# Key rows of a routed attention: one-hot products on TensorE replaced by indirect DMAs driven by token lists

## What is computed

```
s = xn + sum over 8 heads of relu(causal scores)/512 @ V      (stage A)
local = windowed attention, 16 heads of 64, windows of 64      (stage B)
per window w = 1..7, per group g = 0, 1:                       (stage C)
    score the 64*w earlier tokens, keep the 128 best (router: 20 descent steps, then top_k)
    score the window's own 64 tokens, keep the 32 best as queries
    routed = x[b, sel_idx]                   # the selected rows
    out = attention(queries, [null key] + routed rows), 16 heads
    scatter-add out to the queries' tokens
y = (local + scattered) / counts
out = x + s * silu(y)
```

## Time and profile before

| | |
|---|---|
| median of 3 runs | 795.33 us (795.16 to 795.91) |
| profiled execution | 795.43 us, of which the traced span is 793.6 us |
| PE busy | 751.6 us, 95% of the span |
| DVE / ACT / POOL busy | 458.8 / 431.0 / 233.0 us |
| chain that ended last | PE 86%, ACT 5%, DVE 4% |
| granted TensorE clock, mean | 0.991 |
| `a_diag`, `a_v` on DVE (L1512, L1507), mean of 32 each | 692 ns, 692 ns |
| a unit of stage A in head 6, from PE's first scores to the next (174.97 to 181.11) | 6.14 us |
| the query round's two operations (56x64), mean | 224 and 208 ns |

### The profile page before, as it was taken

One profiled execution on the slowest core, in us unless ns is written; L12 is line 12 of the kernel. 1 busy time (PEld: TensorE's weight loads), 2 busy tenths in 40 slices (PEclk: granted clock), 3 DMA queues, 4 the chain that ended last, 5 costly groups with the idle time before them and its releaser, 6 DMA issues.

```text
span 793.6 us, 18031 instructions
## 1 busy us (share of the span) xinstructions
PE 751.6 (95%) x6307; PEld 589.4 (74%) x6311; DVE 458.8 (58%) x1028; ACT 431.0 (54%) x1575; POOL 233.0 (29%) x373
## 2 busy tenths in 40 slices
PE   3799999999999899999999999799999999999996
PEld 3587888878877566666666678687878788787875
DVE  6422333356645788777777752756564555656454
ACT  2254444432223567777766773666474656647562
POOL 1320000000003797554554421422223222212301
PEclk9999999999999999999999998999999999999999
DMA  8600000000001323333333310000000000000001
GB/s 242 273 1 2 0 0 0 0 0 0 0 1 44 92 58 85 91 76 77 76 81 80 76 37 1 1 1 1 0 0 0 1 1 2 1 0 0 0 1 54
DMA packets 22543, 28.87 MB, mean 36 GB/s; under 512 B 6224, under 2 KB 12880, under 8 KB 21840
## 3 DMA queue, kind: packets, MB, share of 16 engines
q1 hardware_dynamic: 22480, 28.04, 12.9%
HBM read 10.19 MB, written 1.05 MB: 14 GB/s over the span
## 4 chain that ended last, share of the span: by engine, by line
PE 86%; ACT 5%; DVE 4%; SPq 2%; issue 2%; POOL 1%; DVEq 0%; DMA 0%; POOLq 0%; ACTq 0%
PE ps L710 9%; PE ps L698 8%; PE ps L759 7%; PE ps L973 6%; PE ps L1033 6%; PE ps L1016 6%; PE ps L1000 5%; PE ps L884 4%; PE ps L832 4%; PE ps L870 4%; PE ps L685 4%; PE ps L957 4%; PE ps L679 3%; PE ps L858 3%; PE ps L895 3%; PE ps L1009 2%
## 5 line engine op out<-in xcount | busy, mean ns | idle before, releaser
L532 POOL TENSOR_TENSOR early<-stage 128x512 f32<-128x512 f32 x64 | 82.7, 1314 | 73.3 <-DVE stage L1586 63.9
L1321 ACT ACTIVATE early<-ps,nmC 128x128 f32<-128x128 f32 (+1 forms) x224 | 78.0, 368 | 44.6 <-DVE dnC L1685 43.9
L1261 ACT ACTIVATE stage<-ps,nmB 128x128 f32<-128x128 f32 x256 | 90.2, 380 | 14.3 <-DVE nmB L1622 12.5
L710 PE MATMUL ps<-stage 128*128 128x128 f32 (+2 forms) x448 | 86.0, 320 | 1.9 <-DVE stage L1512 1.8
L698 PE MATMUL ps<-stage,early 128*128 128x128 f32 (+2 forms) x448 | 86.4, 321 | 0.0
L698 PEld LDWEIGHTS ps<-stage,early 128*128 128x128 f32 x448 | 65.2, 191 | 24.5 <-issue 15.5
L710 PEld LDWEIGHTS ps<-stage 128*128 128x128 f32 x448 | 65.3, 191 | 12.8 <-issue 2.6
L1507 DVE COPY stage<-ps 128x512 f32<-128x512 f32 x32 | 22.1, 692 | 86.3 <-PE ps L685 86.3
L582 POOL TENSOR_SCALAR stage<-iota,kvcol 128x128 f32<-128x128 f32 x112 | 66.1, 606 | 6.7 <-issue 6.7
L1207 ACT ACTIVATE stage<-ps 128x512 f32<-128x512 f32 x64 | 31.4, 491 | 65.1 <-PE ps L698 65.1
L1680 DVE TENSOR_REDUCE nmC<-ps 128x4 f32<-128x512 f32 (+1 forms) x56 | 36.5, 652 | 51.7 <-PE ps L1000 51.6
(11 more groups left out here) (198 smaller groups left out, 1582.3 us busy)
## 6 DMA issues: line engine op xcount, KB each, us to landing
early<-early SPq DMA_DIRECT2D x256, 64.0 KB, 2.0
x<-in_x SPq DMA_DIRECT2D x4, 256.0 KB, 3.9
stage<-in_cq SPq DMA_DIRECT2D x1, 1024.0 KB, 6.3
stage<-in_ck SPq DMA_DIRECT2D x1, 1024.0 KB, 8.3
stage<-in_cv SPq DMA_DIRECT2D x1, 1024.0 KB, 10.3
stage<-in_co SPq DMA_DIRECT2D x1, 1024.0 KB, 12.3
early<-in_wqk SPq DMA_DIRECT2D x1, 1024.0 KB, 14.9
out<-stage SPq DMA_DIRECT2D x4, 256.0 KB, 2.3
```

The source lines that it names most:

```text
L532: pool.tensor_tensor(to, a, b, (ALU.subtract, ALU.add)[f]).then_inc(rot_in, 1)
L710: t = pe.matmul(ps[:, b, q0:q1], vN[:, b % 2, m, :], simA[:, b % 2, s, at:at + q1 - q0], start=False, stop=False, skip_group_check=True)
L1261: t = act.activation(pB[:, u % 2, at, :], ps[:, 4 + h, i * P:(i + 1) * P], ACT.Exp, bias=nmB[:, u % 2, at:at + 1], accum_out=rsB[:, u % 2, ...
L1321: act.activation(pC[:, k, hg, 0:n], ps[:, 5 + k, hg * P:hg * P + n], ACT.Exp, bias=nmC[:, k, hg:hg + 1], accum_out=rsC[:, k, hg:hg + 1])
```

## The change

The codes become token lists, and the one-hot products go.

* The SP queue writes the normed tokens (`xhat`, 1 MB) to a DRAM tensor `xrows` after all loads are issued.
* DVE's `number` now gives each chosen token of the 40 key rows its position (iota, so 1 to 448) and every other token 0. Then 16 more rounds (`position`) take the eight largest positions, write them into a list of 128 and clear them. A last small operation adds the sequence's base. The loop over heads 5 and 6 is written out, and the 36 slots of heads 5, 6 and 7 (three per unit) carry 16 picks, `number`, 16 position rounds and the base.
* PE turns the lists once by one small transpose instead of four (`code_columns`); DVE casts them to integers (`chosen`).
* GpSimd issues 40 indirect DMAs of 128 rows of 512 bytes into a buffer XF: group 0's one per unit in units 0 to 19 of stage B; group 1's in the last units, 5 + 5 + 10, when the rotary buffers under them are free.
* In stage C GpSimd only copies XF[k] to XN[k] (`fetch`). PE's `gather`, ACT's `gathered` and GpSimd's `onehots` are gone; `turn` writes to the start of its PSUM bank.
* Two constants differ: `iota` is 128x448 instead of 128x128, and `base` is one DMA more.

```diff
@@ SP
+            sp.wait_ge(s_xhat, 1)
+            sp.dma_start(xrows.rearrange("(c p) d -> p c d", p=P), xhat[:]).then_inc(s_rows, 16)
@@ GpSimd
+            def gather(g, b, k):
+                at = kv_row(k + 1, g, b)
+                pool.indirect_dma_start(XF[:, (1 - g) * B + b, k - 1, :], None, xrows,
+                                        bass.IndirectOffsetOnAxis(ap=chosen[:, at:at + 1], axis=0)).then_inc(gathered[g], 16)
...
+            pool.wait_ge(s_rows, 16)
+            pool.wait_ge(w_in, W_W2C + 8)
             for u in range(NU):
...
                 if u < B:
                     pick_columns(u)
+                if u == 0:
+                    pool.wait_ge(chosen_in, 1)
+                if u < B * KV_SETS:
+                    gather(0, u // KV_SETS, 1 + u % KV_SETS)
+                if u + 4 >= NU:
+                    if u + 4 == NU:
+                        pool.drain()
+                    for k in range(KV_SETS):
+                        gather(1, u + 4 - NU, 1 + k)
...
-            def onehots(g, b, it, k):
-                at_least(pool, gx_out, it * 6 + k - 1)
...
+            def fetch(g, b, it, k):
+                at_least(pool, cax_out, (it - 1) * WQ + k + 2)
+                rows = (xhat[:, bass.ds(b * BLK, 1), :] if k == 0 else
+                        XF[:, bass.ds(b + (1 - g) * B, 1), k - 1, :])
+                pool.tensor_copy(XN[:, k, :], rows.rearrange("p o d -> p (o d)")).then_inc(xn_in, 1)
             def sequence(g, b, it, before):
+                if isinstance(b, int):
+                    pool.wait_ge(gathered[g], 16 * B * KV_SETS)
+                for k in range(KV_SETS + 1):
+                    fetch(g, b, it, k)
@@ PE
-            def gather(b, it, k):
-                at_least(pe, xt_in, it * 6 + k)
-                if k > 0:
-                    at_least(pe, oh_in, it * 5 + k)
-                n = 1 if k == 0 else (k + 3) // 2
...
             def turn(it, k):
+                at_least(pe, xt_in, it * 6 + k)
                 at_least(pe, xn_in, it * 6 + k + 1)
@@ ACT
-            def gathered(it, k):
-                act.wait_ge(gx_out, it * 6 + k + 1)
-                act.activation(XN[:, k, :], ps[:, 4, 0:D], ACT.Copy).then_inc(xn_in, 1)
@@ DVE
+            def position(i):
+                eight = slice(8 * i, 8 * i + 8)
+                dve.max(RE[kvrows, eight], RS[kvrows, :])
+                dve.drain()
+                dve.match_replace(RS[kvrows, :], RE[kvrows, eight], RS[kvrows, :], 0.0)
+                dve.drain()
+            def choose(slot):
+                if slot < NKV // 8:
+                    pick(kvrows, CTX)
+                elif slot == NKV // 8:
+                    number()
+                elif 0 <= slot - FIRST_POSITION < NKV // 8:
+                    position(slot - FIRST_POSITION)
+                elif slot == FIRST_POSITION + NKV // 8:
+                    dve.tensor_scalar(RE[kvrows, 0:NKV], RE[kvrows, 0:NKV], base[kvrows, 0:1], None,
+                                      ALU.add).then_inc(codes, 1)
```

More of the change, by code:

```diff
@@ L93, in shape_constants @@
     c["eps"] = np.tile(np.stack([1.0 / e, e]).astype(f)[None], (P, 1, 1))
-    c["iota"] = np.tile(np.arange(1, P + 1, dtype=f), (P, 1))
+    c["iota"] = np.tile(np.arange(1, CTX + 1, dtype=f), (P, 1))
+    c["base"] = np.zeros((P, 1), f)
+    for b in range(B):
+        for g in range(G):
+            for w in range(KV_W0, WQ):
+                c["base"][kv_row(w, g, b)] = b * N - 1
     h4, qq = np.arange(P) // NQ, np.arange(P) % NQ
@@ L98, in shape_constants @@
     return c
-CONSTS = ["ident", "causal", "cos", "sin", "window", "rmask", "rinvk", "half", "eps", "iota", "own", "fold"]
+CONSTS = ["ident", "causal", "cos", "sin", "window", "rmask", "rinvk", "half", "eps", "iota", "base", "own", "fold"]
 def build(nc, dram, out):
@@ L132, in build @@
         eps = sb("eps", [P, 2, NITER])
-        iota = sb("iota", [P, P])
+        iota = sb("iota", [P, CTX])
+        base = sb("base", [P, 1])
         own = sb("own", [P, H])
@@ L435, in _ @@
             sp.dma_start(nkv[:], dram["null"]).then_inc(s_const, 16)
-            tiles = [causal, cos, sin, windowf, rmask, rinvk, half, eps, iota, own, fold]
+            tiles = [causal, cos, sin, windowf, rmask, rinvk, half, eps, iota, base, own, fold]
             for name, t in zip(CONSTS[1:], tiles):
@@ L1560, in head @@
                         descend(4 * h + b)
-                    if picks:
-                        pick(slice(0, KV_ROWS), CTX)
-                        if b % (UNITS * PICK_UNITS // (NQ // 8) // UNITS) == 0:
+                    if late is not None:
+                        choose(3 * (late * UNITS + b) + 2)
+                        if late == 0:
                             pick(qrows, W)
-                    if last:
-                        if b == 0:
-                            number()
-                        else:
-                            sums(b - 1)
+                    if last and b > 0:
+                        sums(b - 1)
             head(0, first=True, steps=True)
@@ L1573, in _ @@
             exponents()
-            with dve.Fori(STEP_HEADS, HA - 1) as h:
-                head(h, picks=True)
-            head(HA - 1, last=True)
+            head(STEP_HEADS, late=0)
+            head(STEP_HEADS + 1, late=1)
+            assert STEP_HEADS + 2 == HA - 1 and NQ // 8 == UNITS
+            head(HA - 1, late=2, last=True)
             def b_rope(s):
```

98 lines of the change are left out of this document (36 added, 62 removed).

## The result

The changed kernel took 802.83 us (median of 11 runs, 799.21 to 812.49), the kernel before 795.33 us beside it. The ratio is 1.0083, with a 95% interval of 1.0064 to 1.0103. The ratio leaves out the execution of 812.49 us, which is over 1.5% above the fastest of this kernel. The forecast was 784.0, its range 777 to 794: wrong, and on the other side. The profiled execution took 803.66 us, its span 801.8.

A forecast was written before the change was run, and what follows sets the result against it. PE was taken to bound stages B and C, until DVE's chain binds in stage C. 795.4 + 0.6 startup - 0.4 + 0.9 top-k and seam + 5.0 early indirect DMAs - 17.6 stage C = 783.9, forecast 784.0 us, range 777 to 794.

The forecast's parts named there:

- Eight iterations give 17.6 us: Stage C without one-hot products: 2.3 us less in each of seven iterations, 1.5 in the first, 17.6 us in all.
- rival 5: Stage C: DVE's chain does not bind, so PE's whole 29.8 us come off, 772 us; chance 0.05.
- Startup, top-k and the seam of A and B, +1.1: Before stage B: startup +0.6 us, smaller `number` -0.4, DVE's later readiness at the end of stage A +0.9.
- g, I take 1.2: One indirect DMA's time on GpSimd, 1.2 us, the middle between 0.43 and 1.91; early stage B then costs 5.0 us.
- The formula: Early stage B, g being a DMA's GpSimd time: PE waits 3g at unit 6, 5g - 1.0 in all by unit 8.
- rival 1: Dear descriptors: an indirect DMA holding GpSimd beyond 1.68 us makes the kernel slower, 801 us at 1.91; chance 0.13.
- From unit 8 on g fits in: Stage B from unit 8: GpSimd waits 1.94 us a unit for ACT, so an indirect DMA costs nothing there.
- The last 20: with 1.2 it costs nothing: End of stage B: GpSimd has room for 1.23 us per indirect DMA before stage C's first transpose, so no loss.
- rival 2: Cheap descriptors: an indirect DMA takes GpSimd 0.43 us, the early term is 1.3 us, the time 780; chance 0.12.
- The two signs: Forecast wrong if an indirect DMA holds GpSimd 1.7 us or more, or stage C's iteration falls under 1.1 or over 3.
- Rival 3, DVE's norm: Stage B: indirect DMAs stretch DVE's norm, 16 units lose 0.3 us each, 789 us; chance 0.13 together with Rival 4.
- Rival 4, DVE holds descriptors up: Stage B: a norm delays a DMA up to 0.69 us, early five 3.5 us more, 787.5; chance 0.13 with Rival 3.

The follow-up runs named there:

- experiment 1: Changed kernel without its 40 indirect DMAs, XF cleared by two GpSimd memsets and a drain in place of the wait for them; 780.91 us, ratio 0.9827.
- experiment 4: Changed kernel with group 1's twenty indirect DMAs in the first iteration of stage C, ten ahead of the clearing of oT and ten behind; 809.57 us, ratio 1.0163.
- experiment 9: On experiment 7, group 0's indirect DMAs moved back to units 0 to 19 of stage B; 790.84 us, ratio 0.9938.
- experiment 3: Changed kernel with group 0's indirect DMAs in units 8 to 27 of stage B instead of 0 to 19; 797.71 us, ratio 1.0020.
- experiment 7: On experiment 3, group 1's indirect DMAs issued singly behind GpSimd's copies in iterations 1 to 3 of stage C; 781.35 us, ratio 0.9817.
- experiment 12: On experiment 7, group 1's indirect DMAs as two rows of ten behind the sixth copy of iterations 1 and 2; 798.80 us, ratio 1.0028.
- experiment 13: On experiment 12, each row of ten becomes twenty plain GpSimd DMAs of 128 rows of 256 bytes; 778.46 us, ratio 0.9769.
- experiment 14: On experiment 12, each row of ten parted in the middle by a memset and a drain; 784.24 us, ratio 0.9840.
- experiment 8: On experiment 7, group 1's indirect DMAs as four rows of five behind the sixth copy of iterations 0 to 3; 785.49 us, ratio 0.9861.
- experiment 10: On experiment 9, GpSimd's query-column picks moved from units 0 to 3 to units 20 to 23; 782.57 us, ratio 0.9838.
- experiment 11: On experiment 3, each of group 1's twenty indirect DMAs fetches 64 rows instead of 128; 798.88 us, ratio 0.9991.

## Why the prediction was wrong, step by step

* **"Eight iterations give 17.6 us"**: right. In experiment 1 six iterations give 13.4, the rest 1.7 and the seam, which holds the first iteration, 2.4: 17.5 us. (The changed kernel's own last part is 1.6 us longer than in all but one of the others, at a clock of 0.95 against 0.99 in experiment 1.) DVE's chain binds in the last part, so rival 5 is out.
* **Startup, top-k and the seam of A and B, +1.1**: the marks give -1.5 in the profiled execution and -0.7 to +1.1 in the fourteen others, so the sign isn't settled; the size was at most 1.
* **"g, I take 1.2"**: this is the term that was mis-sized, in what it counted. The DMA's own row is 0.94 to 1.49 us. What it costs GpSimd's queue in the first units is 2.4, because the drain behind it waits too. The formula stands: 3g is 7.2 at g = 2.4 for unit 6 (7.0 measured, in experiments 4 and 9 as well) and 5g - 1 is 11.0 for unit 8 (11.4 measured, 10.5 and 10.1 in 4 and 9). Up to unit 10 another 1.7 are lost, and 1.2 later, which makes the 14.2 us. So it was rival 1 here, with the wrong name: not a dear instruction, but a wait behind it. My bounds, 0.43 and 1.91, came from rows of issues, and none from the gap behind one.
* **"From unit 8 on g fits in"**: right, by experiment 3, where a DMA and the drain behind it fit into what GpSimd had waited for ACT and DVE.
* **"The last 20: with 1.2 it costs nothing"**: this step failed outright. GpSimd's time was right (1.24 us each, the fetches in time). I counted only GpSimd's queue, and a row of indirect DMAs stops the other engines (the wait that the sum had at nothing): 9 us at the seam against before, 10 to 11 against experiments 7 and 1. Experiments 12, 13 and 14 show that in mid-iteration it takes more than five indirect ones without a pause; 7 and 8 that single ones cost nothing, and fives nothing in mid-iteration. What is late are PE's semaphore updates. No rival had it; rival 2, cheap descriptors, is out by the rows. About half of the price is PE's halved clock after the standstill, a term that the sum did not have.
* **How the miss adds up**: against the forecast the seam is 10.5 us longer, the first units 9.2, the last part 2.1 and stage C's six iterations 0.4; the start is 2.6 shorter. The two signs that I had named for a wrong forecast, an indirect DMA of 1.7 us or more and an iteration that falls by less than 1.1 or more than 3 us, both failed to warn: the row is 0.94 to 1.49 us and an iteration falls by 2.2.
* **Rival 3, DVE's norm**: not seen as a loss. The norm's mean in stage B rose (0.82 us against 0.75 before), and PE still kept 7.0 us a unit in experiments 3 and 10 with a DMA in each.
* **Rival 4, DVE holds descriptors up**: a DMA took 0.94 us with DVE idle and up to 1.49 us in stage B, so at most 0.55 us each by the rows, a part of the early term. The Trainium skill, SBUF — State Buffer, SBUF: two separate sides, has a DVE operation that works with both ports shut GpSimd out of descriptor writing; the lengths do not speak against it, no experiment took DVE's work away, and the standstill, with DVE idle, is not this.

What stays open is how the indirect DMAs make PE's semaphore updates late. The ends of products are modelled in the profile, so the trace does not tell whether the product itself is held up or only its signal. That in the same code the loss comes in some executions and not in others (experiment 11's two heaps, 8 us apart, and experiment 3 spreads as widely) was not explained either, nor was a threshold between five and ten looked for.

## What to carry to other kernels

Price a new kind of instruction by its row, by what the next drain on its engine waits, and by what the other engines do meanwhile; a bound taken from other instructions' lengths covers only the first. Indirect DMAs from GpSimd were free when they stood singly in a unit where GpSimd had 2 us or more to spare, and cost 9 us where twenty stood as five, five and ten at the seam, or 8.7 us for each ten in a row in mid-iteration: spread them, move other work of that queue out of their way, and the same change gains 1.8% instead of losing 0.8%. When several engines idle at once and the DMA engines are a fifth busy, look at what the one busy engine issues.

## What the runs showed of the hardware

* An indirect DMA of 128 rows of 512 bytes holds GpSimd for 0.94 us in a row of them, with 0.30 us between two; one of 64 rows 0.90 us; a plain DMA of 128 rows 0.53 us (2.64 for five, 10.70 for twenty).
* A drain behind a DMA issued on GpSimd, with one copy between them, waits 0.5 to 3.0 us, plain or indirect: in the middle 1.4 us in units 0 to 19, where GpSimd works without a break at first, and 0.6 in units 8 to 27 (experiment 3), where it waits in between; with a rotary sum between them 0.23 us.
* Ten indirect DMAs in a row (12.4 us) add 8.7 us to an iteration of stage C, five nothing there and 4.1 us at the seam, twenty plain ones nothing.
* Beside ten in a row PE's semaphore updates are recorded up to 11.2 us after the end of their product, beside none at most 0.14 us; DVE's and GpSimd's are never more than 0.02 us late.
* A standstill of PE by such a row is followed by a granted clock of 0.50: for 10.2 us in experiment 12, where the same 185 products keep PE busy for 36.0 us instead of 31.0.
